# Stores of a convolution kernel issued from ScalarE's queue, a t2 half behind a copy and a seed, and a first memset in two pieces

## What is computed

```python
t1 = p1_w * x                                  # p1_w: one factor per channel and row
t2 = x + t1
t4 = relu(x)
t5 = unfold(x, 3, 7, 1, 1, 1, 3)               # 21 taps of every channel
t7 = einsum('oc,nchw->nohw', p7_w, t4)
t8 = unfold(t7, 1, 5, 1, 3, 0, 6)              # 5 columns, 3 apart
t12 = (x[:, :, None] - t8).mean(2)
t10 = grouped 1x1 convolution of t2 by p10_w (4 groups, c -> 21 c)
t11 = einsum('nck,nmk->ncm', t1, t5) / sqrt(h * w)
t13 = einsum('ncm,nmk->nck', t11, t10) / sqrt(21 c)
return maximum(t13, t12)
```

## Time and profile before

| | |
|---|---|
| median of 3 runs | 395.06 us (395.03 to 396.93) |
| profiled execution, its own time | 392.89 us |
| span of its trace | 391.1 us |
| TensorE busy | 382.6 us (98%) |
| VectorE busy | 330.9 us (85%) |
| ScalarE busy | 254.1 us (65%) |
| GpSimd busy | 91.6 us (23%) |
| DMA | 88.80 MB, 227 GB/s on average |

### The profile page before, as it was taken

How to read it: one execution, slowest core, us unless ns; L and a number is a source line. 1 busy time by engine, 2 the same in 40 slices (tenths; PEclk the granted TensorE clock), 3 DMA queues, 4 the chain that set the end, 5 groups by cost and what they waited for, 6 DMA issues and landing times.

```text
span 391.1 us, 10230 instructions
## 1 busy us (share of the span) xinstructions
PE 382.6 (98%) x4022; PEld 172.2 (44%) x4022; DVE 330.9 (85%) x400; ACT 254.1 (65%) x721; POOL 91.6 (23%) x77
## 2 busy tenths in 40 slices
PE   7999999989999999999999999999999999999996
PEld 3233563353833347333653337433373334732383
DVE  7998999999788896888968888788868889688645
ACT  3425478579577683777656773777827768377790
POOL 1634200822022212222022220222202222122300
DMA  8999116983977757775667937779377783453115
GB/s 294 372 367 415 38 50 260 390 316 111 315 258 256 270 175 238 264 261 196 200 220 252 334 116 224 228 271 318 125 262 238 246 305 110 158 195 109 54 56 215
DMA packets 28704, 88.80 MB, mean 227 GB/s; under 512 B 3312, under 2 KB 3824, under 8 KB 28656
## 3 DMA queue, kind: packets, MB, share of 16 engines
q1 hardware_dynamic: 28656, 88.14, 64.4%
HBM read 71.35 MB, written 16.78 MB: 225 GB/s over the span
## 4 chain that ended last, share of the span: by engine, by line
PE 84%; DVE 6%; DMA 5%; ACT 2%; issue 1%; SPq 0%; DVEq 0%; ACTq 0%
PE ps_y L811 37%; PE ps_y L910 13%; PE ps_t L833 11%; PE ps_p L833 11%; PE ps_y L822 8%; DMA out<-base 3%; DMA xw<-x_conv 2%; DVE pair_sum L635 2%; PE ps_y L1055 1%; DVE box L643 1%; ACT t L398 1%; PE ps_y L833 1%; PE ps_t L811 0%; DVE v_planes L564 0%; DVE v_planes L559 0%
## 5 line engine op out<-in xcount | busy, mean ns | idle before, releaser
L811 PE MATMUL ps_y<-v_planes,u_planes 64*64 64x512 f32 x1488 | 184.1, 594 | 0.4 <-DVE v_planes L564 0.3
L290 POOL TENSOR_TENSOR t1T<-t1T,p1T_sb 128x512 f32<-128x512 f32 x64 | 84.4, 1341 | 267.6 <-PE ps_y L822 212.1
L398 ACT ACTIVATE t<-xn,p_plus 128x64 f32<-128x64 f32 x512 | 127.9, 335 | 0.0
L833 PE MATMUL ps_t<-t,aT 64*64 64x512 f32 x440 | 113.3, 590 | 0.1
L833 PE MATMUL ps_p<-box,p_fifth 64*64 64x512 f32 x424 | 109.0, 589 | 2.5 <-ACT ps_p L322 2.5
L811 PEld LDWEIGHTS ps_y<-v_planes,u_planes 64*64 64x64 f32 x1488 | 56.8, 133 | 110.7 <-issue 103.7
L625 DVE STREAM_TRANSPOSE yT<-ps_y 128x512 f32<-128x512 f32 x62 | 40.7, 695 | 30.5 <-PE ps_y L822 30.1
L322 ACT ACTIVATE base<-ps_p 128x512 f32<-128x512 f32 x55 | 32.8, 596 | 50.6 <-PE ps_p L833 45.9
L910 PEld LDWEIGHTS ps_y<-t1T,yT 128*128 128x128 f32 x448 | 50.5, 192 | 5.7 <-issue 5.7
L910 PE MATMUL ps_y<-t1T,yT 128*128 128x128 f32 x448 | 51.9, 277 | 0.0
L659 DVE TENSOR_TENSOR base<-ps_t,base 128x512 f32<-128x512 f32 x56 | 38.4, 687 | 12.2 <-PE ps_t L833 11.9
(11 more groups left out here) (74 smaller groups left out, 221.0 us busy)
## 6 DMA issues: line engine op xcount, KB each, us to landing
xw<-x_conv SPq DMA_DIRECT2D x63, 561.0 KB, 6.6
xn<-x_nat SPq DMA_DIRECT2D x32, 512.0 KB, 4.5
t1T<-x_pix SPq DMA_DIRECT2D x32, 512.0 KB, 5.0
out<-base SPq DMA_DIRECT2D x63, 256.0 KB, 4.8
u_planes<-w_tiles SPq DMA_DIRECT2D x4, 336.0 KB, 6.2
out<-base SPq DMA_DIRECT2D x2, 128.0 KB, 2.0
p1T_sb<-p1T SPq DMA_DIRECT2D x1, 128.0 KB, 7.6
p_sb<-p7T SPq DMA_DIRECT2D x1, 64.0 KB, 7.7
```

The costliest lines, as they stand in the source:

```text
L290: nc.gpsimd.tensor_tensor(part, part, p1T_sb[:, e, :].unsqueeze(1).broadcast_to([P, 4, C]), ALU.mult).then_inc(t1_ready, 1)
L398: last = nc.scalar.activation(t2[:, h, W * r:W * (r + 1)], xn[:, f, at:at + W], ACT.Copy, scale=p1_plus[:, 8 * h + r:8 * h + r + 1])
L811: last = nc.tensor.matmul(dst[TILE * pair:TILE * pair + TILE, :], weights_of(rows_of(half), u, weights, TILE * k, TILE), data_of(rows_of(h ...
L833: last = nc.tensor.matmul(dst[cols, 0:data.shape[-1]], weights[rows, cols], data[rows, :], start=start, stop=False, skip_group_check=True)
```

## The change

Three things. (1) All stores of images 0 to 5 and the first two of image 6 (h = 0, 1) are issued by ScalarE, between its activations, in ScalarE's own DMA queue; the other stores of the last two images stay in SP's queue, behind all loads. Of h = 2 to 7 of an image, ScalarE issues them one image later in its program (n-2 in the loop below), h = 0 and 1 earlier (n-1). (2) In the slot of unit 5, `t2_half(0, 4)` comes behind `base_half(0, 5)` and `seed_x(0, 6)`. (3) relu_pad[:, 1] is cleared in two memsets (7 rows of 76, then 9), and the zero products use the first alone.

```diff
+ZERO_ROWS = 7
@@ SP, loop over n @@
                 load_natural(n, 0)
-                store(n - 2, 4)
-                store(n - 2, 5)
                 load_natural(n, 1)
                 load_group(u + 4)
-                store(n - 2, 6)
                 load_pixels(n)
                 load_natural(n, 2)
-                store(n - 2, 7)
                 load_group(u + 5)
-                store(n - 1, 0)
-                store(n - 1, 1)
                 load_natural(n, 3)
                 load_group(u + 6)
-                store(n - 1, 2)
-                store(n - 1, 3)
-            for h in range(4, 8):
+            for h in range(2, 8):
                 store(LAST - 1, h)
@@ ScalarE @@
+            def store(n, h):
+                act.wait_ge(out_ready, 8 * n + h + 1)
+                act.dma_start(out[n, :, h * HALF:(h + 1) * HALF], base[:, h, :]).then_inc(stored[h], 16)
...
             t2_half(0, 3)
-            t2_half(0, 4)
             base_half(0, 5)
             seed_x(0, 6)
+            t2_half(0, 4)
             t2_half(0, 5)
             base_half(0, 6)
             seed_x(0, 7)
+            store(0, 0)
 
             copy_two(6)
             relu(1, 1)
             t2_half(0, 6)
             base_half(0, 7)
             seed_x(1, 0)
+            store(0, 1)
...
                 t2_half(n - 1, 2 - 2 * late)
+                store(n - 2, 2)
                 base_half(n - 1, 1)
                 seed_x(n - 1, 2)
+                store(n - 2, 3)
...
                 t2_half(n - 1, 4 - 2 * late)
+                store(n - 2, 4)
                 base_half(n - 1, 3)
                 seed_x(n - 1, 4)
+                store(n - 2, 5)
...
                 t2_half(n - 1, 6)
+                store(n - 2, 6)
                 base_half(n - 1, 5)
                 seed_x(n - 1, 6)
+                store(n - 2, 7)
                 t2_half(n - 1, 7)
                 base_half(n - 1, 6)
                 seed_x(n - 1, 7)
+                store(n - 1, 0)
 
                 copy_two(u + 2)
                 t2_half(n, 0)
                 base_half(n - 1, 7)
                 seed_x(n, 0)
+                store(n - 1, 1)
@@ VectorE, TensorE @@
-            nc.vector.memset(relu_pad[:, 1], 0.0).then_inc(zeroed, 1)
+            nc.vector.memset(relu_pad[:, 1, 0:ZERO_ROWS], 0.0).then_inc(zeroed, 1)
+            nc.vector.memset(relu_pad[:, 1, ZERO_ROWS:], 0.0).then_inc(zeroed, 1)
-            zeros = relu_pad[:, 1].rearrange("p a b -> p (a b)")
+            zeros = relu_pad[:, 1, 0:ZERO_ROWS].rearrange("p a b -> p (a b)")
```

## The result

The changed kernel takes **392.29 us** (median of 8 runs, 391.81 to 393.71), the kernel before 395.04 in the same comparison (8 runs, 393.85 to 396.93). The ratio is 0.9928, 95% interval 0.9903 to 0.9954: 0.7% faster, 2.75 us, and more than the forecast's 0.3 us. The interval leaves 1.8 to 3.8 us; three later comparisons have the kernel before at 394.16, 394.93 and 394.40, so 395.04 is the highest of its medians. The two profiled executions are much closer: 392.36 and a span of 390.6 us, against 392.89 and 391.1. That gap between 0.53 and 2.75 us is what the experiments had to explain.

The account below looks back on a forecast made before the run. TensorE was taken to bound the kernel, idle only in image 0's outputs; 0 + 0 per image - 0.3 took the profiled 392.89 to 392.6 and the median 395.06 to 394.8 us, own range 394.2 to 395.3, wide 392.8 to 396.2.

Parts of the forecast that it names:

- What bounds the kernel now, and its ceiling: TensorE bounds; only its idle time in image 0's outputs can be won, 0.92 + 1.74 = about 2.7 us at most.
- The two holes: TensorE idle 0.72 us ahead of 63.50 (order of ScalarE's work) and 1.74 ahead of 80.10 (store(0,0) landing late).
- The zeros: At the start, splitting the first memset: value 0, bounds -0.1 to +0.1 us.
- The rows of t2: Image 0's outputs: with t2_half(0,4) later, the idle time near 63 us goes whole, p7 rows 0.92 us sooner.
- The stores in ScalarE's queue: store(0,0) lands in 2.0 to 4.8 us, the 1.74 us wait goes; issues take 0.4 us, costing 0 per image.
- What is late next: Near 79 us, VectorE and GpSimd alternating on a lock hold t13(0,4) until 79.4; TensorE wins only 0.3 us.
- Rival (a): Near 79 us, VectorE is not in the way: TensorE wins 1.2 to 2.7 us, 392.3 to 393.9; chance 0.17.
- Sum: 0 + 0 per image - 0.3: profiled execution 392.89 to 392.6; on the median of 395.06, 394.8.
- Rival (b): VectorE loses the lock race at 69.4; GpSimd's fifth product precedes box_pairs: 0.9 us slower, 396.0; chance 0.14.
- (c): Stores don't overtake the loads, store(0,0) lands at 78.8: no change, 395.1 (394.7 to 395.4); chance 0.09.
- (d): Every image: stores land later than 5.5 us or an issue costs over 0.85; 401 at a 6.6 landing; chance 0.08.

Follow-up runs that it names:

- g2: The kernel before, unchanged, profiled once more: 395.21 us in that profiled execution, with a fall of the clock.
- g1: The kernel before, unchanged, profiled once more: 393.41 us in that profiled execution, without a fall of the clock.
- e4: The kernel before with only the first memset cut in two pieces: 395.30 us, ratio 1.0020.
- e5: The change without its memset part: 392.18 us, ratio 0.9931 to the kernel before.
- e3: The kernel before with only t2_half(0,4) moved behind the copy and the seed, stores in SP's queue: 395.34 us, ratio 1.0019.
- e6: The kernel before with the new order of t2 and only store(0,0) and store(0,1) in ScalarE's queue: 392.09 us, ratio 0.9924.
- e8: The kernel before with image 1's loads of unit 8 and t1T moved ahead of load_natural(1,1), nothing else: 391.43 us, ratio 0.9910.
- e7: The change with image 1's loads of unit 8 and t1T moved ahead of load_natural(1,1): 390.44 us, ratio 0.9889 to the kernel before.
- e2: The kernel before with only the stores moved to ScalarE's queue, old order of t2, one memset: 395.19 us, ratio 1.0006.
- f1: The change with five extra copies of ps_p7 to a spare tile ahead of base_half(1,0): 392.04 us, ratio 0.9941 to the kernel before.
- e1: The kernel before once more, unchanged, for a second trace and more times: 394.33 us, ratio 1.0003.
- f2: The change with seven extra copies of ps_p7 to a spare tile ahead of base_half(1,0): 394.48 us, ratio 0.9983 to the kernel before.
- g4: The kernel before, unchanged, profiled once more: 394.69 us in that profiled execution, with a fall of the clock.
- f3: The kernel before, unchanged, profiled once more: 393.20 us in that profiled execution, without a fall of the clock.
- f4: The kernel before, unchanged, profiled once more: 392.99 us in that profiled execution, without a fall of the clock.

## Why the prediction was wrong

**What bounds the kernel now, and its ceiling.** The two holes and their causes were right. "That is the ceiling: 0.92 + 1.74 = about 2.7 us, and no more" was wrong: it counts the idle time of one execution, not what follows from a stop. From taps to taps the two holes of that very execution cost 1.05 + (11.92 - 9.84) = 3.1 us, and in four of eight traces the stop brought a fall of the clock, worth 1.3 us more in g2 than in g1.

**The zeros.** Forecast 0. e4 gives no change (1.0020) and e5, without that part, is as fast as the whole: right.

**The rows of t2.** Forecast p7 rows at 62.6 instead of 63.50; they start at 62.66. Right: every trace with this order has 9.83 or 9.84 us from taps to taps there, every one without it 10.88 to 10.92, so it brings 1.05 us where 0.92 was forecast. e3 has them too, but behind them its stop for the store is longer, and its median is no better; that the longer stop is what takes them back is argued from one trace.

**The stores in ScalarE's queue.** Right that base_half(1,0) would be released by TensorE, and right by e6 that the later stores cost nothing. "The second hole of 1.74 us would go as well" held for the wait for the seed alone; the stretch went from 11.92 to 12.31 us, which the next part of the prediction foresaw in kind. Mis-sized: the landing took 7.0 us, not 2.0 to 4.8, and in e8 it took 6.8 in a shorter SP queue, so a queue of its own bought no more than a shorter one. The issue takes 0.34 us in the queue and, by the rows at 66.22 to 66.75, nothing from ScalarE, the lower bound.

**What is late next.** Right almost to the row: box_last first, GpSimd in every turn, box_pairs at 76.12 for 2.39 (76.4 plus a turn), max_half(0,3) ending at 79.11 (79.3 to 79.4), t13(0,4) at 79.25 (79.4), stop released by VectorE. Rival (a), by which VectorE was not in the way, would have given 392.3 to 393.9; the median, 392.29, lies at its edge, and the trace refutes its mechanism. e7 shows the lock to be the cause: without GpSimd there, no stop is left. t13(0,5) starts at 84.78 where 85.1 was forecast.

**Sum.** This step failed. On the profiled execution it gave 392.6, and 392.36 came: 0.53 won where 0.3 was forecast. Then it said: "The median of the runs shown is 395.06, 2.2 above it; on it, 394.8." It carried over as a constant what was not one: the term of 2.2 us was taken to stay, and most of it went with the change. As far as the traces show, it is the second hole's own doing. By the table of eight, in five of them the store lands 0.2 to 0.5 us later, GpSimd wins the race for the lock by some hundredths to 0.3 us and the stop is 2.0 to 2.2 instead of 1.7 us; in four of the five the clock falls. The change takes away what this hangs on. The store is not waited for, and GpSimd's products run on without a pause, so box_pairs always takes 2.39 us and this race is not open any more; the stop of 1.01 us was followed by a fall in none of the profiles of the change, e5 and e6. Against g2 the changed kernel wins 1.04 us ahead of the single taps (76.24 against 75.20) and 14.16 - 12.31 = 1.85 behind them, 2.9 in all; against g1 it wins 1.05 in all and against the quickest 0.53. The 2.75 measured is a median over executions of all these kinds.

Rival (b) told of this very race, in the changed kernel. It had put the margin there at 0.12 us and had not seen that before's own margin, 0.13 us in the earlier trace rows, was as thin. e2 shows its mechanism at work: with the stores alone box_pairs takes 2.40 and nothing is won. Rivals (c) and (d) did not come about.

**What stays open.** Over 54 timed executions of before beside these kernels, 17 show a mean clock of 0.996 or less, and they took 394.6 to 397.2 us; of 23 executions of the change, e5, e6 and f1, none does. So in most executions the clock does not fall. The 37 of before with a full clock took 392.76 to 395.82 us with a median of 394.01, which is 1.7 us over the change, and 31 of them took more than 393.41, the longest profile at full clock. So the race and the clock account for 0.5 to 2.9 us execution by execution, but in more than half of all executions of before something is lost, typically 394.01 - 393.41 = 0.6 us, that no trace shows. An earlier stop like e8's at 44.18, worth 1.58 us, is a poor candidate: it lies ahead of everything that the change edits, and yet 22 of those 23 executions took 391.75 to 392.64 us (the other 393.71). Nor is it shown why the landing goes from 11.84 to 12.37, what decides that a stop of 2.08 us (g1) is not followed by a fall and one of 1.91 (e2) is, or why e7 took 389.5 twice and then 391.38 and, with a mean clock of 0.996, 391.82; its profile is of the first kind. Why a load of xw is sometimes over a microsecond late is not shown either.

## What to carry to other kernels

Before a trace is set against a median, ask what in it could have gone the other way: two requests for one lock 0.1 us apart, or a transfer that lands a few tenths before it is wanted, make a kernel with several times, and the profile shows one of them. If the profiled execution is far below the median, the difference is a thing to find and not a constant to add; several profiles of the same kernel find it. A stop of TensorE is to be priced from one fixed point of the program to the next and not by its idle time, for work that runs alone instead of side by side costs as well, and so does what follows the stop; two edits that each leave one stop standing can be worth nothing alone and the whole together. And where one engine's work holds another by a lock, look where the load that releases that work stands: moving it here brought as much as the whole change, or more.

## What the runs showed of the hardware

- Eight stops of 1.91 to 2.92 us were followed by TensorE's granted clock at 0.50 for some 3.4 us, 1.7 us of full speed lost (e1 to e4, f2, g2 to g4); stops of 0.71 to 1.87 us were not (f1, f3, f4, e3, e8, the changed kernel), and one of 2.08 (g1) was not either. Of ten executions of f2, whose profiled stop is 2.85, three kept the full clock.
- The products of p7 and of t13, each on 64*64 of TensorE, ran side by side (76.69 and 76.70 in e7, 0.60 us each); in the changed kernel, where t13's came late, the stretch took 2.45 us longer with only 1.01 us idle.
- Where GpSimd and VectorE both have two-input additions to do, they take turns: 0.72 becomes 1.79 us and 1.32 becomes 2.38 to 2.42 on VectorE, 1.28 becomes 2.3 on GpSimd. Which asks first was decided by 0.01 to 0.32 us.
- A store of 256 KB landed in 11.22 to 12.37 us at the end of SP's queue (e3, and the eight of before), in 6.8 to 7.2 on ScalarE's empty one with the same loads in SP's (e2, the change, e5, e6), and in 6.8 in SP's where less stood ahead of it (e8). ScalarE issued it in 0.34 to 0.38 us while an activation ran.
